# Expert attention in 32 units of (tile, routing slot) instead of 64 of (tile, expert)

## What is computed

```python
def _L0_ffn_ref(x, router_w, router_b, wq, bq, wk, bk, wv, bv, wo, bo):
    probs = jax.nn.softmax(x @ router_w + router_b, axis=-1)
    _, top2 = jax.lax.top_k(probs, 2)
    for e in range(e_total):                       # 4 experts
        member = (top2 == e).any(-1)
        ...                                        # the members' rows in xg, their weights in wg
        q = (xg @ wq[e] + bq[e]).reshape(b, s, h, hd)     # 16 heads of 8
        ...                                        # k and v in the same way
        att = jnp.einsum('bqhd,bkhd->bhqk', q, k) * 0.5
        att = jnp.where(validg[:, None, None, :], att, -1000000000.0)
        y = jnp.einsum('bhqk,bkhd->bqhd', softmax(att), v) @ wo[e] + bo[e]
        out = out.at[bidx, order].add(wg[..., None] * y)
```

## Time and profile before

| what | value |
|---|---|
| time, median of 3 launches | 1146.18 us (1145.13 to 1148.81) |
| profiled execution, span | 1173.7 us |
| its mean granted clock of TensorE | 0.937 |
| TensorE busy | 1028.9 us, 88% of the span |
| VectorE busy | 719.7 us, 61% |
| ScalarE busy | 572.7 us, 49% |
| GpSimd busy | 455.1 us, 39% |

### The profile page before, as it was taken

One profiled execution on the slowest core, in us unless ns is written; L12 is line 12 of the kernel. 1 busy time (PEld: TensorE's weight loads), 2 busy tenths in 40 slices (PEclk: granted clock), 3 DMA queues, 4 the chain that ended last, 5 costly groups with the idle time before them and its releaser, 6 DMA issues. The chain is left out here.

```text
span 1173.7 us, 30389 instructions
## 1 busy us (share of the span) xinstructions
PE 1028.9 (88%) x12369; PEld 776.1 (66%) x12369; DVE 719.7 (61%) x1421; ACT 572.7 (49%) x1152; POOL 455.1 (39%) x518
## 2 busy tenths in 40 slices
PE   5899999998687779999999999997899787837994
PEld 4788888887465657777777666664366556525873
DVE  3455555555275478888888888884589487301324
ACT  2455555554253246666676656664455364402120
POOL 1232233232253425544444654422244483370143
PEclk9999999999898779999999999998999798767997
DMA  8300060000000100000000000003952100111235
GB/s 252 131 1 1 1 182 1 1 1 1 1 1 1 37 1 3 3 3 3 3 3 2 3 3 2 2 2 122 377 150 73 38 4 2 51 56 32 57 110 166
DMA packets 42104, 55.26 MB, mean 47 GB/s; under 512 B 3088, under 2 KB 33424, under 8 KB 41584
## 3 DMA queue, kind: packets, MB, share of 16 engines
q1 hardware_dynamic: 39984, 49.07, 13.6%
q0 software_dynamic: 1984, 4.26, 1.1%
HBM read 30.13 MB, written 23.19 MB: 45 GB/s over the span
## 5 line engine op out<-in xcount | busy, mean ns | idle before, releaser
L1583 ACT COPY e_PT<-probsT 128x512 f32<-128x512 f32 x192 | 103.7, 588 | 123.2 <-PE probsT L1431 123.2
L1592 ACT ACTIVATE e_P<-e_P 128x512 f32<-128x512 f32 x192 | 111.3, 633 | 5.0 <-DVE e_P L1689 4.0
L1431 PE MATMUL probsT<-W,e_P 128*128 128x128 f32 x768 | 105.3, 280 | 9.1 <-ACT e_P L1592 9.1
L539 POOL TENSOR_TENSOR c_P<-c_P,c_rl 128x1024 f32<-128x1024 f32 x32 | 60.7, 1897 | 127.9 <-DVE c_rl L679 127.9
L1686 DVE TENSOR_REDUCE e_mx<-scores 128x16 f32<-128x1024 f32 x64 | 78.3, 1224 | 25.1 <-PE scores L1419 23.8
L1431 PEld LDWEIGHTS probsT<-W,e_P 128*128 128x128 f32 x768 | 84.2, 142 | 14.2 <-ACT e_P L1592 11.3
L676 DVE TENSOR_REDUCE c_rl<-c_P 128x8 f32<-128x1024 f32 x32 | 39.0, 1220 | 81.9 <-ACT c_P L363 81.9
L576 PEld LDWEIGHTS misc<-c_xs,c_AQ 128*128 128x128 f32 x488 | 62.3, 194 | 35.0 <-issue 33.5
L1249 POOL TENSOR_TENSOR e_RK<-e_Ks,W 128x512 f32<-128x512 f32 x64 | 66.1, 1042 | 46.3 <-PE scores L1419 26.9
L1689 DVE TENSOR_TENSOR e_P<-scores,e_mx 128x1024 f32<-128x1024 f32 x64 | 78.4, 1225 | 6.9 <-DVE e_mx L1686 0.5
L1444 PEld LDWEIGHTS mixed<-e_Vbd,e_PT 128*64 128x64 f32 x2048 | 64.9, 138 | 25.6 <-issue 19.3
(11 more groups left out here) (373 smaller groups left out, 2341.6 us busy)
## 6 DMA issues: line engine op xcount, KB each, us to landing
hbm_dist<-u_Z SPq DMA_DIRECT2D x16, 768.0 KB, 9.0
u_S<-hbm_dist SPq DMA_DIRECT2D x64, 128.0 KB, 2.9
hbm_results<-c_blank SPq DMA_DIRECT2D x1, 3072.0 KB, 14.5
e_w<-in_w SPq DMA_DIRECT2D x12, 256.0 KB, 2.6
e_dT<-hbm_results SPq DMA_DIRECT2D x12, 256.0 KB, 3.9
W<-in_wpack SPq DMA_DIRECT2D x1, 2489.0 KB, 12.8
hbm_slots<-c_blank SPq DMA_DIRECT2D x6, 350.0 KB, 6.3
e_xin<-hbm_slots SPq DMA_DIRECT2D x6, 350.0 KB
```

The source lines that it names most:

```text
L539: pool.tensor_tensor(pr, pr, bc(rl[:, a.up, :].unsqueeze(2), [P, PAIRS, KEYS]), ALU.mult).then_inc(s["scaled"], 1)
L1431: last = pe.transpose(K.psT[:, i * P:(i + 1) * P], Pr[:, n % 2, i * P:(i + 1) * P], K.ident)
L1583: act.copy(PT[:, n % 2, half * 512:(half + 1) * 512], K.psT[:, half * 512:(half + 1) * 512]).then_inc(s["tcopied"], 1)
L1592: act.activation(Pr[:, n % 2, cols], Pr[:, n % 2, cols], ACT.Exp, scale=0.5 if n < TOTAL else CSCALE).then_inc(s["exped"], 1)
```

## The change

A token has two experts, so a unit becomes (tile, routing slot k), n = 2 t + k: 32 units. wq and wk are laid out anew in the first stage (GpSimd), so that the 32 rows of a head hold four experts with eight dimensions each; a group of 128 rows has four heads. Queries are multiplied by a one-hot mask (`selT`) of the expert that the token has in slot k, so that the contraction over expert and dimension leaves the chosen expert's score. Keys are written once per tile, in pairs of heads (64 rows, `RK` 128x1024). The mask of the keys is the product of `selT` and `neg`, over 64 rows. The array works as 64x64 tiles: four mask products of 512 columns and 16 score products of 128 columns a unit. The scores lie in `psS[0]`; the mix goes to `psS[1]`: 16 products of 66 columns (two heads, four experts' values and the sum). The normalisation multiplies by 1/sum and by the router's weight of the chosen expert (`fac`), 512 columns; the two slots are added on GpSimd. Projections are made two tiles ahead, queries and keys in the two units of a tile; the key bias moves from VectorE to ScalarE (four evictions), the values and the output transposes from `M` to `psO`. At the start of the stage 48 small bf16 products spread the one-hot rows over heads and dimensions. In the first stage 32 small DMAs bring the biases into the new layout. The fourth block's first three tiles are transposed at once, and its second scores wait for `psS[1]`.

```diff
...
+                for i, name in enumerate(("bq", "bk")):
+                    for j in range(4):
+                        for e in range(E0):
+                            sp.dma_start(K.biasE[32 * j + 8 * e:32 * j + 8 * e + 8, i, :],
...
+                def spread_heads(name, n):
+                    wait(pool, s["heads"], n)
+                    every = w(name).rearrange("p (e g j d) -> p g j e d", e=E0, g=4, j=4)
+                    for g in range(4):
+                        last = pool.tensor_copy(byhead[:, g, :, :, :], every[:, g, :, :, :])
...
+                    for i, name in enumerate(("wq", "wk")):
+                        if a.n == 16 + 4 * i:
+                            spread_heads(name, 2 * i)
+                        if a.n == 18 + 4 * i:
+                            gather_heads(name, 2 * i + 1)
...
-            U, TOTAL, TILE_S = E0, TILES * E0, 1
+            U, TOTAL = TOPK, TILES * TOPK
+            Qs, RK = sb("Qs", [P, 2, TOPK, 4, P]), sb("RK", [P, 2, 4, TB, 2, S])
+            mixed = lambda n: (K.psS[1] if n < TOTAL - 1 else K.psOM.rearrange("p b c -> p (b c)")).rearrange(
+                "p (h c) -> p h c", c=S)
...
+                    def select(t):
...
+                        pool.wait_ge(s["qout"], t + 1)
+                        if t == 0:
+                            pool.wait_ge(q["selout"], 1)
+                        wait(pool, s["scored"], U * (t - 1))
+                        for k in range(TOPK):
+                            pool.tensor_tensor(Qs[:, t % 2, k, :, :], QT[:, :, :],
+                                               bc(selT[:, t, k, :].unsqueeze(1), [P, 4, P]), ALU.mult).then_inc(s["qin"], 1)
...
+                        pool.tensor_tensor(o[:, t % 2, 0, :, :], o[:, t % 2, 0, :, :], o[:, t % 2, 1, :, :], ALU.add).then_inc(
+                            s["summed"], 1)
...
+                        if u == 0:
+                            if t >= 1:
+                                keys(t + 1)
+                            biases(t - 1)
+                        else:
+                            add_slots(t - 1)
+                            select(t + 2)
...
+                        slots(0, K.psT)
+                        outside(0, K.psS[0])
+                        slots(1, K.psS[1])
+                        pe.wait_ge(q["selout"], 1)
+                        slots(2, K.psT)
+                        pe.wait_ge(q["selout2"], 1)
+                        slots(3, K.psS[1])
+                        pe.wait_ge(q["selout"], 3)
+                        outside(2, K.psT)
...
                         wait(pe, s["shifted"], n)
-                        pe.wait_ge(s["qout"], t + 1)
-                        pe.wait_ge(s["kbd"], n + 1)
...
+                        pe.wait_ge(s["qin"], n + 1)
+                        half = lambda g: slice(64 * g, 64 * g + 64)
+                        bank = lambda g, b: K.psS[0][half(b), 512 * g:512 * g + 512]
+                        for b in range(TB):
+                            for g in range(2):
+                                pe.matmul(bank(g, b).rearrange("p (h k) -> p h k", h=8), selT[half(g), t, k, half(b)],
+                                          bc(neg[half(g), t, half(b)].unsqueeze(1), [64, 8, S]), start=True, stop=False,
+                                          skip_group_check=True)
+                        pe.wait_ge(s["kin"], t + 1)
+                        for h in range(4):
+                            for b in range(TB):
+                                for g in range(2):
+                                    last = pe.matmul(bank(g, b)[:, 128 * h:128 * h + 128], Qs[half(g), t % 2, k, h, half(b)],
+                                                     RK[half(g), t % 2, h, b, :, :].rearrange("p j k -> p (j k)"), start=False,
+                                                     stop=True, skip_group_check=True)
...
+                        wait(pe, s["normed"], n if n < TOTAL - 1 else n - 1)
+                        if k == 0:
+                            wait(pe, s["xsum"], t - 1)
                         for i in range(PAIRS):
+                            g, pair = i // 4, 2 * (i % 4) + i // 4
                             for b in range(TB):
...
+                                last = pe.matmul(mixed(n)[64 * b:64 * b + 64, 2 * pair:2 * pair + 2, 0:E0 * HD + 1],
                                                  PT[:, n % 2, i * P + 64 * b:i * P + 64 * b + 64],
-                                                 Vbd[:, t % 2, u, i, b, :, :], start=True, stop=True)
+                                                 Vbd[:, t % 2, b, pair, :, :], start=True, stop=True)
...
+                        if n == 1:
+                            pe.wait_ge(s["normed"], TOTAL - 1)
+                            pe.wait_ge(s["xsum"], TILES - 2)
...
                         score(n + 1) if n + 1 < TOTAL else wide_score(0)
...
+                            queries(t + 2)
+                            out(t - 2)
+                            mix(n - 1)
+                            turn(n)
+                        else:
+                            keys(t + 2)
+                            mix(n - 1)
+                            oturn(t - 1)
+                            turn(n)
                             values(t + 1)
...
+                        for g in range(4):
+                            last = act.activation(KT[:, g, :], M[:, g * P:(g + 1) * P], ACT.Identity, bias=K.biasE[:, 1, g:g + 1])
...
+                        if u == 0:
+                            if t >= 1:
+                                keys(t + 1)
+                            outT(t - 2)
                         tcopy(n - 1)
...
                         exp(n)
+                        if u == 0 and t >= 1:
+                            values(t)
...
+                        dve.tensor_tensor(fac[:, n % 2, :, :], bc(rl[:, n % 2, :].unsqueeze(2), [P, HEADS, E0]),
+                                          bc(wsel[:, t, k, :].unsqueeze(1), [P, HEADS, E0]), ALU.mult).then_inc(s["factor"], 1)
...
                         shift(n)
                         normalise(n - 2)
                         if u == 1:
-                            queries(t + 1)
...
+                            queries(t + 2)
+                            finish(t - 2)
...
```

More of the change, by code:

```diff
@@ L1384, in queries @@
                             return
-                        wait(pe, s["oTc"], t - 2)
-                        for e in range(E0):
-                            last = pe.matmul(M[:, e * P:(e + 1) * P], w("wq", e * D, D), xs(t), start=True, stop=True)
+                        wait(pe, s["kout"], t)
+                        for g in range(4):
+                            last = pe.matmul(M[:, g * P:(g + 1) * P], w("wq", g * P, P), xs(t), start=True, stop=True)
                         last.then_inc(s["q"], 1)
@@ L1393, in keys @@
                         pe.wait_ge(s["qout"], t + 1)
-                        for e in range(E0):
-                            last = pe.matmul(M[:, e * P:(e + 1) * P], w("wk", e * D, D), xs(t), start=True, stop=True)
+                        for g in range(4):
+                            last = pe.matmul(M[:, g * P:(g + 1) * P], w("wk", g * P, P), xs(t), start=True, stop=True)
                         last.then_inc(s["k"], 1)
@@ L1564, in _ @@
[L1564 removed]
+                        if n == 0:
+                            wide_score(1)
+                            out(TILES - 2)
+                            mix(TOTAL - 1)
+                        else:
+                            wide_score(n + 1)
+                            wide_mix(n - 1)
                         turn(TOTAL + n)
[L1566 removed]
+                        if u == 0 and FIRST <= t + 2 < TILES:
@@ L1601, in wide_outT, with keys @@
                         act.copy(coT[:, :], M[:, 0:P]).then_inc(c["oTc"], 1)
+                    def keys(t):
+                        if t >= TILES:
+                            return
+                        act.wait_ge(s["k"], t + 1)
+                        wait(act, s["kin"], t)
+                        for g in range(4):
+                            last = act.activation(KT[:, g, :], M[:, g * P:(g + 1) * P], ACT.Identity, bias=K.biasE[:, 1, g:g + 1])
+                        last.then_inc(s["kout"], 1)
                     def values(t):
```

374 lines of the change are left out of this document (212 added, 162 removed).

## The result

The changed kernel takes 1086.78 us (median of four launches, 1082.82 to 1088.84), the kernel before 1147.49 us beside it (four launches, 1145.13 to 1149.93): a ratio of 0.947, 95% interval 0.944 to 0.950. The saving is 60.7 us.

What follows compares the result with a forecast made beforehand. TensorE's own order was taken to bound the tile: 11.1 us of slots plus 0.5 of waits, 11.6. With start, thirteen tiles, end and 3 us hand-over, 59 us saved: 1146.2 - 59 = 1087, range 1072 to 1108.

Steps and rivals of the forecast that it cites:

- The slot sum: TensorE in one loop tile: two units of scores, mix and transposes, plus projections, wo, values, output transposes: 11.1 us.
- The waits: In the loop, TensorE's waits for other engines, including the held factor product: 0.5 us charged, making 11.6 a tile.
- The two places "with no room": In each loop tile, key projection waits for VectorE's query bias and values for ScalarE's output-transpose copy, without slack.
- The start: Start of the stage at 1.2 GHz: first maximum at 430.2, 9.5 us later than before; 6 if the clock rises earlier.
- T0 of tile 1: Start of scores(2t+1) for t = 1, after two latency-bound units: at 442, then thirteen tiles of 11.6 us.
- The end: Loop end: last two tiles 9.6 us, 4.4 to the wide stage's first scores at 607, maximum at 608.6.
- The hand-over: Border to the wide stage: second wide scores wait for the PSUM half that normalise(30) frees; 3 us charged.
- Neighbours pace the tile: Rival, 20%: in the loop, key projection or values come 1 to 1.5 us later; tile 12.6 to 13.1, time 1103 to 1111.
- Tiles take turns: Rival, 6%: the 64x64 array tiles do not overlap in scores; scores 2.0 us, 21 us more, 1108.
- The rule behind it: Skill's rule for TensorE: a weight load overlaps running matmuls only where row groups differ; scores near 2.0 a unit, 1108.
- Slower by the clock: Rival, 3%: loop at 1.2 GHz, each slot doubled, 11 us a tile; 1175 with half the loop at that level.
- More saved: Rival, 5%: masks hidden, start only 6 us late, tile 10.9 us; time 1074 or below.

Runs made afterwards that it cites:

- the experiments on VectorE and ScalarE: Two edits of the changed kernel: VectorE's query bias addition done twice per tile, 1089.08 us; ScalarE's four key evictions done twice per tile, 1090.18 us.
- the second execution: The changed kernel run again unaltered, on the chip of the second version of the reordered stage start: 1085.83 us, ratio 0.947 to the kernel before.
- the two orders that alternate rows or columns: Changed kernel with its sixteen score products per unit reordered: neighbours share rows and alternate columns, 1095.14 us; share columns and alternate rows, 1100.06 us.

## Why the prediction was right

Forecast 1087.0 with a range of 1072 to 1108, measured 1086.78.

- **TensorE's order sets the tile.** Right, and more strictly than put: 65.00 of 65 us busy, and the kernel without masks returns what it takes from TensorE.
- **The slot sum.** 11.1 predicted, 11.16 measured. Scores 1.35 against 1.22 (products 0.98 where I had 1.1), mix 1.09 against 1.08, values 1.0 against 1.01, transposes 0.9 against 0.97 and 1.02, projections 0.99 against 0.99 and 1.08, output transposes 0.45 against 0.49. The scores were 0.13 too long, transposes and keys about 0.1 too short.
- **The waits.** 0.5 charged, nothing paid in the steady loop. The two places "with no room" are the right ones, the experiments on VectorE and ScalarE make a wait there; but they have 0.2 to 0.3 and 0.75 us. The factor product is held as predicted, 1.75 instead of 0.22, and nobody waits for it. This is the mis-sized term: 13 tiles of 0.44 are 5.7 us. With a first tile of 10.4 the 13 took 144.3 us (444.78 to 589.06) in place of 150.8.
- **The start.** First maximum at 430.2 predicted, 430.54 in the profile; from the beginning of the stage 28.1 us before, 36.5 and 39.1 in two executions after, so 8.4 to 10.9 later. The sum is right, its parts are not. The first spread ended at 417.5 and not at 419.0: I took the steps ahead of it at half the clock throughout, and it rose to 0.90 for 4 us. From there to the end of the last spread it took 7.7 us and not 4.5 (425.21): I put the time on the chain of spreads and their evictions, and missed that the query bias waits for GpSimd's slot products (4.5 us, with an eviction behind it). The first scores then took 1.4 and not 2.7, at a granted clock of 0.84 from 428 to 432. The three cancel, and that they do is luck.
- **First tile of the steady loop.** T0 of tile 1 at 442 predicted, 444.8 measured: 2.8 late. From the first maximum it is 14.2 us where 11.8 were summed, at a granted clock of 0.59 and 0.56 from 432 to 440; in the second execution, at 0.99 and 1.00 there, it is 12.0 (433.66 to 445.71). The sum of the units was right, and the clock is what it lacked.
- **The end.** First wide maximum 608.6 predicted, 606.3 measured. From scores(29) at 589.06 to the first wide scores at 604.61 it took 15.5 us where 14.0 were charged: the three normalisations that VectorE has to make there, beside GpSimd's work, stood in no term, and TensorE waits 1.25 us behind them. The hand-over: 3 charged; from the first to the last wide maximum it is 119.6 in place of 118.1, so 1.5, and 121.2 in the second execution, so 3.1. The mechanism is there: the second wide scores start at 610.04 behind the normalisation that ends at 609.99, 1.28 late.
- **The saving.** From the beginning of the stage to its last wide maximum 396.4 before (392.56 to 789.0) and 331.9 after (394.02 to 725.9): 64.5 against 59. The last stage's first product starts 61.9 earlier (1005.27 and 943.40), as this execution came to the changed stage 1.5 later and lost some 1 us behind it; the medians show 60.7. Against the forecast the 13 tiles were 6.5 shorter, the hand-over 1.5, and the stage began 1.5 later than counted; the loop's start was 2.8 too cheap and its end 1.5. So the mechanism and its size were right, and differences of a few us between executions did the rest: that the forecast came within 0.3 us is luck.
- **The profile of 1115.** Wrong by 34. The step that failed was to carry the saving from the span of an execution that is 27.5 us longer than the median: the surplus was a last stage 30.8 us longer, of no concern to the change, and would have been seen there.
- **The rivals.** Neighbours pace the tile: no, but by 0.3 us. Tiles take turns: no, shown by the two orders that alternate rows or columns. The rule behind it was put to the wrong order: in the change's order neighbours never share rows, so the changed kernel's own time says nothing about the rule, and 1108 was no price of it. Slower by the clock: no, the loop has 1.00. More saved: the masks were hidden by 0.05 only, the tile was 11.16 and not 10.9.

## What to carry to other kernels

Where one engine's list is busy without a gap, add up its slots from start to start; the others only need room at the places where that list waits for them, and what goes beyond that room is paid, not the whole operation. Before a stage's loop, look for buffers that the loop needs once but the start needs twice, and for the small operations queued behind them: another order at this start was worth 9.5 us, a sixth of what the whole change brought, though its steps were not separated. And where a small VectorE step from SBUF to SBUF takes many times its own time beside GpSimd, ask first who waits for it: here it cost nothing in the loop, 0.6 and 0.3 us at the start and 1.25 at the border with the next block.

## What the runs showed of the hardware

- Products on 64x64 tiles of the array: 0.153 us each where all use one tile, 0.092 where two alternate, 0.061 where four do; it is 0.092 for two tiles that share rows as for two that share columns.
- 32 passes on half-width tiles cost 1.05 us with 18 or 34 columns and 1.08 with 66.
- Some of VectorE's operations from SBUF to SBUF stand still while GpSimd works: the cast of the identity (2.05 beside a memset, 0.22 alone), the outside mask (1.92 beside the key product, 0.22 alone, the latter also in the second execution of the changed kernel), the factor product of two SBUF operands (1.75, 0.22), the softmax's two products (2.19, 0.36), the fourth block's normalisation (three in 3.72, 0.34 each alone). Operations from PSUM keep their time beside the same work: all 32 maxima take 1.19 to 1.23. The Trainium skill (SBUF — State Buffer, SBUF: two separate sides) tells of a lock on a port pair that VectorE and GpSimd share, taken for a whole instruction by VectorE's operations with two SBUF inputs (against GpSimd operations that read SBUF) or in a 2-port performance mode; these rows agree with it, but in which mode the operations of one SBUF input ran, no row shows. The prediction had the effect in the loop, where it cost nothing, and not at the start and at the border, where it did.
- The granted clock at the start of this stage differs from one execution of the same kernel to another (0.90 and 0.50 in 408 to 412 us), and the place of the first maximum with it (36.5 and 39.1 us behind the beginning of the stage); by the last maximum they agree to 0.4 us. What decides it isn't shown by these runs.
